# The sixth round of row gathers: plain copies into a spare buffer, and sixteen adds on two engines

## What is computed

```python
x = x + attention(layernorm(x))
x = x + wkv(layernorm(x), ctx)
xf = layernorm(x)                                  # 2048 tokens of 512
shared = silu_and_mul(xf @ shared_w1.T) @ shared_w2.T
routing_weights, selected = top_k(softmax(xf @ gate_w.T), 6)     # 6 of 16 experts
moe = sum over the 6 chosen experts e of weight_e * silu_and_mul(xf @ w1[e].T) @ w2[e].T
out = x + moe + shared
```

## Time and profile before

| | |
|---|---|
| median of three runs | 2027.1 us (2023.09 to 2030.69) |
| the profiled execution, its own time | 2021.53 us |
| its span in the profile | 2019.1 us |
| TensorE busy | 1897.8 us, 94% |
| GpSimd busy | 1015.7 us, 50% |
| VectorE busy | 1015.5 us, 50% |
| ScalarE busy | 858.7 us, 43% |
| gathers on GpSimd (line 1480) | 96, busy 148.9 us |
| DMA queue of GpSimd (q0) | 51.13 MB |

### The profile page before, as it was taken

The page is one execution under the profiler, slowest core; times in us unless marked ns, Lnnn a source line. Parts: engine busy times, 40 slices in busy tenths (PEclk is TensorE's granted clock), DMA queues, the critical chain, the costliest instruction groups (busy, mean ns, idle before and its releaser), DMA issues. The chain is left out here.

```text
span 2019.1 us, 39259 instructions
## 1 busy us (share of the span) xinstructions
PE 1897.8 (94%) x11084; PEld 1704.5 (84%) x11085; DVE 1015.5 (50%) x2197; ACT 858.7 (43%) x1880; POOL 1015.7 (50%) x1068
## 2 busy tenths in 40 slices
PE   6999999999999999999889977677999999999997
PEld 5888888888888888888778967677999999999896
DVE  4644444444566566665676534333444444444442
ACT  4654444444557566665553102222333333333332
POOL 5544444432444544555572065366344333488886
PEclk8999999999999999999999988888999999999998
DMA  9776767668767777866352267455455444599999
GB/s 328 232 247 231 230 228 230 229 205 312 253 240 269 286 259 261 318 217 246 115 183 94 94 235 220 154 190 188 129 142 162 129 129 129 142 224 223 201 217 247
DMA packets 236927, 422.47 MB, mean 209 GB/s; under 512 B 41232, under 2 KB 98320, under 8 KB 236816
## 3 DMA queue, kind: packets, MB, share of 16 engines
q1 hardware_dynamic: 119408, 310.79, 46.4%
q0 software_dynamic: 21504, 51.13, 10.5%
q10 hardware_dynamic: 95904, 59.15, 10.5%
HBM read 276.13 MB, written 144.83 MB: 208 GB/s over the span
## 5 line engine op out<-in xcount | busy, mean ns | idle before, releaser
L1129 PE MATMUL bank<-w_hi,xT 128*128 x1776 | 480.2, 333 | 3.6 <-DVE xT L1694 3.5
L990 PE MATMUL bank<-w_hi,xT 128*128 128x512 f32 x1024 | 358.6, 411 | 7.8 <-DMA xT<-xT_att 5.8
L1129 PEld LDWEIGHTS bank<-w_hi,xT 128*128 128x128 f32 x1776 | 320.2, 191 | 10.9 <-issue 5.9
L1395 POOL TENSOR_TENSOR rr<-rr,expo 128x4 f32<-128x4 f32 x128 | 129.0, 1007 | 343.4 <-DVE rr L1590 343.1
L1129 PE MATMUL bank<-w_lo,xT 128*128 x888 | 289.0, 325 | 0.0
L1139 PE MATMUL bank<-w_hi,hT 128*128 x666 | 233.2, 405 | 27.5 <-DVE hT L613 20.0
L990 PEld LDWEIGHTS bank<-w_hi,xT 128*128 128x128 f32 x1024 | 196.0, 191 | 52.1 <-issue 7.3
L1694 DVE TENSOR_TENSOR xT<-bank,xT 128x512 fp32r<-128x512 f32 x111 | 76.8, 692 | 267.6 <-ACT xT L1310 227.4
L1014 PE MATMUL bank<-w_hi,xT 128*128 128x256 f32 x1024 | 208.8, 289 | 0.0
L990 PE MATMUL bank<-w_lo,xT 128*128 128x512 f32 x512 | 205.0, 400 | 0.0
L1037 PE MATMUL bank<-w_hi,oT 128*128 128x512 f32 x512 | 192.9, 417 | 0.0
(11 more groups left out here) (239 smaller groups left out, 4055.6 us busy)
## 6 DMA issues: line engine op xcount, KB each, us to landing
xT<-xT_att SPq DMA_DIRECT2D x126, 512.0 KB, 4.7
w_hi<-w_split SPq DMA_DIRECT2D x64, 512.0 KB, 6.2
w_lo<-w_split SPq DMA_DIRECT2D x64, 512.0 KB, 7.1
rows_flat<-blank SPq DMA_DIRECT2D x111, 264.0 KB, 5.3
raw<-in_weights SPq DMA_DIRECT2D x82, 276.0 KB
w_split<-w_hi SPq DMA_DIRECT2D x64, 276.0 KB, 3.5
w_split<-w_lo SPq DMA_DIRECT2D x64, 276.0 KB, 3.9
xT<-xT_ffn SPq DMA_DIRECT2D x32, 512.0 KB
```

What stands on the lines that cost most here:

```text
L990: last = pe.matmul(bank[par][:, :], xT[:, par, a, c * P:(c + 1) * P], w_hl[w][:, fw, c * 512:(c + 1) * 512], start=n == 0, stop=n == 11)
L1129: last = pe.matmul(out_[:, 0:I], xT[:, par, a, c * P:(c + 1) * P], flat(w_hl[w])[:, bass.ds(at + (c * CW + half_ * (I + E)), I)], start=n ...
L1395: pool.tensor_tensor(rr[:, :], rr[:, :], expo[:, :], ALU.pow).then_inc(pw_done, 1)
```

## The change

Rounds 0 to 4 stay. In round 5 the 16 gathers no longer add: they copy the rows into `xnB[:, b, 0:512]`, which nobody reads any more, and so they do not wait for the fifth round either. The sum is made by two engines: GpSimd, behind its last gather, adds tiles 0 to 11 (`xres += xnB`), VectorE, behind its last block, adds tiles 12 to 15. SyncE's stores wait for these adds (`hold_done` for GpSimd's, `added` for VectorE's) in place of the gathers.

```diff
         ROUTE_AT = 20
+        POOL_ADDS = 12
         COUNT_AT = 22
...
                 for b in range(B):
-                    sp.wait_ge(g_in[b], 16 * TOPK)
+                    if b < POOL_ADDS:
+                        sp.wait_ge(hold_done, 2 * TOPK + b + 1)
+                    else:
+                        sp.wait_ge(added, NSH + b - POOL_ADDS + 1)
                     sp.dma_start(out[b], xres[:, b, :]).then_inc(stored, 16)
...
                     for b in range(B):
-                        wait(pool, g_in[b], 16 * k)
-                        pool.indirect_dma_start(out=xres[:, b, :], out_offset=None, in_=yg[:, :],
-                                                in_offset=bass.IndirectOffsetOnAxis(ap=slot_i[:, k, b:b + 1], axis=0),
-                                                compute_op=ALU.add).then_inc(g_in[b], 16)
+                        if k < TOPK - 1:
+                            wait(pool, g_in[b], 16 * k)
+                            pool.indirect_dma_start(out=xres[:, b, :], out_offset=None, in_=yg[:, :],
+                                                    in_offset=bass.IndirectOffsetOnAxis(ap=slot_i[:, k, b:b + 1],
+                                                                                        axis=0),
+                                                    compute_op=ALU.add).then_inc(g_in[b], 16)
+                        else:
+                            pool.indirect_dma_start(out=xnB[:, b, 0:D], out_offset=None, in_=yg[:, :],
+                                                    in_offset=bass.IndirectOffsetOnAxis(ap=slot_i[:, k, b:b + 1],
+                                                                                        axis=0))\
+                                .then_inc(g_in[b], 16)
...
                 gather_add(4)
                 gather_add(5)
+                for b in range(POOL_ADDS):
+                    pool.wait_ge(g_in[b], 16 * TOPK)
+                    pool.tensor_tensor(xres[:, b, :], xres[:, b, :], xnB[:, b, 0:D], ALU.add).then_inc(hold_done, 1)
...
                 sparse(dve, block_step)
+                for b in range(POOL_ADDS, B):
+                    dve.wait_ge(g_in[b], 16 * TOPK)
+                    dve.tensor_tensor(xres[:, b, :], xres[:, b, :], xnB[:, b, 0:D], ALU.add).then_inc(added, 1)
```

## The result

The changed kernel takes 2032.83 us in the median of 20 runs (2018.34 to 2040.58), the kernel before 2023.50 us in the median of 20 (2004.17 to 2030.69). The ratio is 1.0046 with a 95% interval of 1.003 to 1.0062: slower by 6 to 13 us, about 9. The profiled execution has a span of 2032.4 us against 2019.1. Of these 13.3 us, 5.8 lie ahead of the sixth round of gathers, which starts at 1981.48 in place of 1975.65 although nothing is changed there; executions of one kernel differ by that much. From here on I therefore count from the **start of the sixth round**. To the end of the span it was 43.4 us before and is 50.9 us now: 7.5 us more, where 1.7 were forecast.

The account below looks back on a forecast made before the run. Taken as bound: GpSimd's gather issue, landing, SyncE's last store. Issue -9.4, GpSimd's adds +15.2, contention +2.4, landing and SyncE's wait -9.7 + 0.2, stores +3.0: +1.7 on 2027.1 gives 2028.8 us; range 2022.5 to 2038.

Parts of the forecast that it names:

- the first rival: Sixth round's plain gathers still issue every 1.855 us, as adding ones do: +10.5 us, 2037.6 us; chance 0.18.
- step 1: GpSimd's sixth round: plain gathers issue every 1.265 us like scatters, the last ending at 1995.6, 9.4 us sooner.
- step 2: Rows of the sixth round's gathers land before their adds, tile 11's by about 1995, so nothing is paid.
- step 3: GpSimd's twelve adds behind its last gather: 1.25 us each, 15.0 us together, from 1995.8 until 2010.8.
- step 4: VectorE, free at 2003.3, makes four adds of about 0.6 us; contention costs GpSimd 2.4 us, ending at 2013.2.
- step 5: SyncE's last stores: tile 11 at 2013.4, four behind it add 3.0 us, a store 4.4; span ends at 2020.8.
- The floor: Adds cost nothing; TensorE's last block, stored at 2008.13, ends the span at 2012.5, -6.6 us; within a 0.05 rest.

Follow-up runs that it names:

- e3: The changed kernel, but the sixth round's gathers into the spare buffer add; ratio 1.0048 to the kernel before.
- e5: The changed kernel with a GpSimd memset of a dead 128x512 buffer ahead of each of the sixteen plain gathers; ratio 1.0008 to the kernel before.
- e7: The kernel before with a small GpSimd power ahead of each scatter of the fourth to sixth rounds; 1994.72 us against 2024.33, ratio 0.9854.
- e9: Kernel before, only tiles 12 to 15 gathered plainly and added by VectorE, three GpSimd products ahead of each scatter in rounds four to six; ratio 0.9799.
- e10: As e9, but with the scatters of all six rounds paced; 1998.98 us, ratio 0.9876 to the kernel before.

## Why the prediction was right, and where it was not

The time (2032.83 us) lies in the range and the change is within 0.5%, as forecast. But the 1.7 us of the forecast became 7.5 in the profile and 9 in the runs, and of the reasons one was missing and one was turned round. That the time was met is in part luck. The sum's 2028.8 is missed by only 4.0 us because it starts from the median of three runs (2027.1), which lies 3.6 us above the median of twenty (2023.50); counted from 2023.50 it would be missed by 7.6. And the upper part of the range was there for the first rival, whose mechanism did not come.

- *Issue of the sixth round* (step 1): right. 19.8 us to the end of the issue, 19.95 forecast; the price is the scatter's, and e3 shows that the add makes the difference.
- *Landing* (step 2): right as to the adds on GpSimd, which run without a gap. GpSimd's queue from 1990 to 1998 gives 0.262 / 1.73 x 5.82 = 0.88 us of all engines for a plain gather, against 1.44 for one that adds and the 0.7 that I took from the scatters:

```profile
q0 software_dynamic: 523, 1.73, 72.8%
```

- *Twelve adds* (step 3): right. They start 19.8 us behind the round's start (20.15 forecast) and come 1.24 us apart (1.25).
- *Four adds on VectorE* (step 4): wrong twice. First, "VectorE is free at 2003.3", 27.65 us behind the round's start. It was free 44.1 us behind it, because TensorE paused; that is the term that the sum lacked. I read TensorE beside adding gathers only (21.0 of 21.0 us busy) and took over their silence for plain ones, while I took the price of plain ones from the scatter rounds. The scatter rounds that gave the price also showed the pause: 14.0 of 30 us busy. Second, "GpSimd loses what VectorE's instruction takes". In the change the adds never met. Where they did, in e3 and e5, GpSimd lost nothing and VectorE stood for 14 us, so the 2.4 us of contention in the sum were not there. The earlier trace rows show VectorE starting first, or at the same moment, each time: they say that two such instructions exclude each other, and not who yields when GpSimd's come without a gap. (L530 overlaps GpSimd's product there by 1071.31 - 1070.28 = 1.03 us, not by 0.95.)
- *The stores* (step 5): the four behind tile 11 were late as the step says, but by VectorE's lateness (9.7 us of waiting), not by their own length. In e3 and e5 the span ends 6.4 us behind GpSimd's last add, where the step has 0.2 + 4.4 + 3.0 = 7.6.
- *The floor*: the rival took 32.5 us behind the round's start for the last block's store. It came at 47.5 and, with 3.5 us of landing, set the end.
- *The first rival* gave 10.5 us more, nearer to the measured 9 than the forecast's 1.7, by a mechanism that did not happen: plain gathers cost 0.95 us and not 1.55.

What the change would bring without the pause is not measured by itself. An estimate from e5, where GpSimd's last add ends at 40.6 and the span at 47.0: the tail behind that add is 47.0 - 40.6 = 6.4 us. With GpSimd's 34.7 us the end would be at 34.7 + 6.4 = 41.1 us, 2.3 less than before.

What stays open is why close issues hold TensorE back. The runs show that it is the spacing (gone at 1.63 to 1.66 us, there at 1.25 to 1.38), for gathers and scatters. Half the bytes changed nothing in one execution, and four in a row did no harm; between four and sixteen nothing was tried. The timeline shows TensorE's signals arriving late, two of them together. Through which path GpSimd's issues delay it was not tried. Nor is it shown why gathers that add, issued 1.86 us apart, are harmless other than by their spacing, since they cannot be issued closer.

## What to carry to other kernels

When a change turns one kind of instruction into another, look in the trace for every place where the new kind already runs, and read there what the *other* engines do, not only what the instruction costs. In this kernel long rows of plain indirect DMAs from GpSimd, issued back to back, held up TensorE: 0.4 us of other work between two of them, best of all work that has to be done, gave 2.8% together with a shorter last round. Where GpSimd itself is waited for, as for the experts' weights, the spacing has its price (e7, e9, e10), so it should be no wider than needed. And where VectorE and GpSimd both have two-input work on SBUF tiles, leave gaps in GpSimd's or keep them apart in time.

## What the runs showed of the hardware that was not expected

- Sixteen plain indirect DMAs issued 1.25 to 1.27 us apart hold up TensorE, VectorE and ScalarE. TensorE's longest pause was 16.0, 6.6 and 7.8 us in the three scatter rounds beside the blocks, and 12.0 and 9.0 us in two executions of the gather round; it ended 3.4 to 4.3 us behind the last issue, and in the gather round the DMA share was 0.71 to 0.74 meanwhile. At 1.38 us apart there are pauses of 4.5 to 7.8 us, at 1.63 us none.
- An indirect gather of 128 rows of 2 KB costs GpSimd 952 ns plain and 1552 ns with the add, into the same buffer.
- VectorE's 128x512 add of two SBUF tiles, 0.68 us alone, took 14.0 us beside GpSimd's adds without a gap, which kept their 1.22 to 1.24 us. The Trainium skill (SBUF — State Buffer, Who interferes with whom) says that such a pair contends; the trace agrees, and adds that here VectorE alone pays.
